# The second cross attention's scores moved from the head of a unit to the middle of the unit before

## The reference

```python
q = (query @ Wq.T + bq).reshape(N, Lq, HEADS, HEAD_DIM).transpose(0, 2, 1, 3)
k = (keys @ Wk.T + bk).reshape(N, Lk, HEADS, HEAD_DIM).transpose(0, 2, 1, 3)
v = (values @ Wv.T + bv).reshape(N, Lk, HEADS, HEAD_DIM).transpose(0, 2, 1, 3)
energy = jnp.einsum('bhqd,bhkd->bhqk', q, k)
energy = jnp.where(mask[:, None, None, :] == 0, jnp.float32(-1e+20), energy)
attention = jax.nn.softmax(energy / np.sqrt(HEAD_DIM), axis=-1)
out = jnp.einsum('bhqk,bhkd->bhqd', attention, v)
return out.transpose(0, 2, 1, 3).reshape(N, Lq, EMBED) @ Wo.T + bo
```

## Time and profile before

| | |
|---|---|
| median of three timed runs | 1763.58 us |
| span of the profiled execution | 1759.1 us |
| median less span | 4.5 us |
| TensorE busy | 1715.7 us, 98% of the span |
| layer 1's cross attention, first scores to last transpose | 1072.4 to 1303.4 us |

### The profile page before, as it was taken

One profiled execution on the slowest core, in us unless ns is written; L12 is line 12 of the kernel. 1 busy time (PEld: TensorE's weight loads), 2 busy tenths in 40 slices (PEclk: granted clock), 3 DMA queues, 4 the chain that ended last, 5 costly groups with the idle time before them and its releaser, 6 DMA issues.

```text
span 1759.1 us, 28411 instructions
## 1 busy us (share of the span) xinstructions
PE 1715.7 (98%) x11211; PEld 1315.8 (75%) x11211; DVE 910.5 (52%) x2029; ACT 716.4 (41%) x1564; POOL 238.3 (14%) x317
## 2 busy tenths in 40 slices
PE   7999999999999999999999999999999899999997
PEld 5677777777757666555999986777758587999997
DVE  4234344434346686523756564665564864455543
ACT  3333333333324436422655554555445442243432
POOL 0100000000003202422111031211101221121112
PEclk9999999999999999999999999999999999999999
DMA  6011010102042003025999961111231312788983
GB/s 248 25 73 48 25 48 25 49 25 96 1 156 96 1 1 144 23 99 214 375 390 390 384 200 60 37 37 31 79 144 35 155 59 96 317 329 325 327 326 94
DMA packets 43666, 245.87 MB, mean 140 GB/s; under 512 B 5786, under 2 KB 6290, under 8 KB 20481
## 3 DMA queue, kind: packets, MB, share of 16 engines
q1 hardware_dynamic: 31248, 215.91, 32.2%
q0 software_dynamic: 7664, 19.68, 4.0%
q10 hardware_dynamic: 4608, 8.33, 1.2%
HBM read 228.29 MB, written 16.13 MB: 139 GB/s over the span
## 4 chain that ended last, share of the span: by engine, by line
PE 92%; DVE 3%; issue 2%; DMA 1%; ACT 1%; POOL 1%; SPq 0%; POOLq 0%; DVEq 0%; ACTq 0%
PE bank L639 29%; PE bank L259 22%; PE bank L265 4%; PE bank L782 3%; PE bank L3284 3%; PE bank L810 3%; PE bank L1971 3%; PE bank L1973 3%; PE bank L1972 3%; PE bank L736 2%; PE bank L2773 2%; PE bank L1473 2%; PE bank L729 2%; PE bank L1157 2%; PE bank L1530 1%
## 5 line engine op out<-in xcount | busy, mean ns | idle before, releaser
L639 PE MATMUL bank<-split 128*128 128x512 f32 x2196 | 539.7, 398 | 0.8 <-ACT arena L665 0.8
L639 PEld LDWEIGHTS bank<-split 128*128 128x128 f32 x2196 | 401.9, 188 | 130.8 <-issue 21.7
L259 PE MATMUL bank<-arena,weights 128*128 128x128 f32 (+1 forms) x1992 | 244.7, 282 | 11.8 <-DMA weights<-in_L_xattn_w_kv 8.8
L259 PEld LDWEIGHTS bank<-arena,weights 128*128 128x128 f32 x1992 | 232.6, 192 | 25.2 <-issue 13.5
L753 DVE TENSOR_REDUCE small<-bank 128x1 f32<-128x512 f32 x64 | 43.9, 686 | 166.1 <-PE bank L729 166.1
L790 ACT COPY normed<-bank 128x512 f32<-128x512 f32 x128 | 68.9, 591 | 125.7 <-PE bank L782 125.7
L671 DVE COPY arena<-bank 128x512 f32<-128x512 f32 x76 | 52.4, 689 | 111.8 <-PE bank L639 111.8
L665 ACT COPY arena<-bank 128x512 f32<-128x512 f32 x76 | 44.6, 587 | 149.2 <-PE bank L639 116.0
L265 PE MATMUL bank<-weights,arena 128*128 128x512 f32 x224 | 102.9, 610 | 0.9 <-issue 0.9
L772 ACT ACTIVATE normed<-bank,small 128x512 f32<-128x512 f32 x64 | 44.1, 690 | 124.0 <-DVE small L755 123.7
L3390 DVE SCALAR_TENSOR_TENSOR arena<-bank,cols,arena 128x128 f32<-128x128 f32 x96 | 30.5, 349 | 114.5 <-issue 67.1
(11 more groups left out here) (397 smaller groups left out, 2915.8 us busy)
## 6 DMA issues: line engine op xcount, KB each, us to landing
weights<-in_L_ffn_re_w SPq DMA_DIRECT2D x62, 1024.0 KB, 8.2
weights<-in_L_w SPq DMA_DIRECT2D x20, 1408.0 KB, 11.0
arena<-in_ctxT SPq DMA_DIRECT2D x24, 1024.0 KB, 4.8
arena<-in_L_w SPq DMA_DIRECT2D x12, 1408.0 KB, 8.9
weights<-in_L_w_full SPq DMA_DIRECT2D x10, 1280.0 KB, 10.4
weights<-in_L_ffn_sw SPq DMA_DIRECT2D x9, 1024.0 KB, 4.9
expert_out<-arena ACTq DMA_DIRECT2D x31, 256.0 KB, 8.2
arena<-in_L_w_full SPq DMA_DIRECT2D x6, 1280.0 KB, 10.2
```

Of the source, the lines that this page charges most:

```text
L259: s = pe.matmul(out, w[:, k, j0:j0 + m], rhs(k), start=(k == 0), stop=(k == KT - 1))
L639: s = pe.matmul(bank[:, :], still, moving, start=(n == 0), stop=(n == len(order) - 1))
```

## The change

TensorE's order of issue alone changes, in layer 1 alone. The scores of unit 0 stand ahead of the loop. The scores of unit n + 1 are issued in unit n, behind the values of unit n - 1 and ahead of the second kv block and the turn of unit n. In layer 0 the scores stay where they were. The other engines' programs, the DMAs, the buffers and the number of instructions are as before.

```diff
@@ -840,8 +840,11 @@
 
             units = len(self.units)
             beside = units - (2 if self.layer == 0 else 3)
+            if self.layer == 1:
+                self.scores_tensor(pe, 0)
             for n, c, u, first, second, third, splits in self.plan:
-                self.scores_tensor(pe, n)
+                if self.layer == 0:
+                    self.scores_tensor(pe, n)
                 self.queries_tensor(pe, self.queries_beside(c, u))
                 for g in first:
                     self.kv_tensor(pe, *g)
@@ -851,6 +854,8 @@
                     project(n - beside)
                 if n >= 1:
                     self.values_tensor(pe, n - 1)
+                if self.layer == 1 and n + 1 < units:
+                    self.scores_tensor(pe, n + 1)
                 for g in second:
                     self.kv_tensor(pe, *g)
                 self.turn_tensor(pe, n)
```

## The result

The changed kernel takes 1758.93 us in the median of 10 runs (1754.85 to 1760.8), the kernel before 1763.75 us in as many (1761.37 to 1774.51). The ratio of the comparison is 0.9959, with a 95% interval from 0.9946 to 0.9971: faster by 7.2 us, between 5.1 and 9.5. The quotient of the two medians is 0.9973; both lie beyond 0.2%. Run again beside 23 runs of the kernel before, the changed kernel gave 0.9952 (0.9938 to 0.9967).

The account below looks back on a forecast made before the run. TensorE, busy 1715.7 of 1759.1 us, was taken as the bound. Savings of 6.2 + 0.9 = 7.1 us, with insertion and waits at zero, gave a span of 1752.0, plus 4.5 for the median: 1756.5 us, range 1754.5 to 1761.0.

Parts of the forecast that it names:

- What bounds the kernel: Layer 1's stage: TensorE busy for all 229.90 us, so only how tightly its blocks follow each other can change.
- Taking the scores out: Between turn and next block, 31 places: saves 0.24 us before kv (26), 0.18 before a float32 block (5), 7.1 us.
- Putting them in behind values: Scores after values in each unit: step out of values 0.58 us, scores 1.06 us, so no added cost.
- bound (+2.5, -1.6 us): Values into scores: 0.08 us more per unit, or 0.05 less if two array forms share part of their switch.
- The rule of the Trainium skill: Changing tiling mode drains TensorE: four changes a unit become three, one drain less in 31 units, estimated at 5.1 us.
- Unit 0: First unit: unit 1's scores cover the turn's 0.19 us softmax wait but split kv from turn; net 0.03 us won.
- The waits: Moved scores, turn, values, queries and keys in layer 1: all waits stay covered, cost 0; scores have 1.05 us of cover.
- Rival C: Scores wait for late maxima, holding back kv and turn: slower, middle 14 us, 1777 us; chance 0.03.
- Rival D: Behind the stage, more stretches at the lower clock give back 3.5 us: 1760.0 us; chance 0.06.

Follow-up runs that it names:

- full-array pair: The kernel before and the changed kernel, each with its scores matmuls on the full array instead of 64x128 halves; stages 244.50 and 244.34 us.
- scores before turn: Changed kernel with the scores of unit n + 1 moved behind the second kv block, ahead of the turn; stage 225.26 us, ratio 0.9971.

## Why the prediction was right, point by point

- *What bounds the kernel.* In the stage TensorE is busy without a pause, before and after. Right.
- *Taking the scores out.* 0.24 us a place with kv: the units shown give 0.23 and 0.21. 0.18 with a float32 block: the turn takes 0.93 for 1.02 (1288.05 - 1287.12 in the trace after) and the projection 3.53 (1291.58 - 1288.05) for 3.64 (1289.10 - 1285.46 in the trace before), 0.20. Sum 7.1 predicted, 6.92 measured, 0.22 for each of the 31. As the full-array pair shows, the split of a place's 0.24 us between turn and kv was not a reading that the rows allow; the sum was.
- *Putting them in behind values.* The value taken from values' other two followers, 0.58 and 1.06, was met. Neither bound (+2.5, -1.6 us) was needed. The full-array pair shows why: the cost goes with the change of form. The step from two measured followers to a third was an extrapolation, and it held.
- *The rule of the Trainium skill* (TensorEngine Tiling (Array Packing), section Key Properties: changing the tiling mode drains TensorE). The traces agree in kind: where the move takes away no change of form, 6.9 us became 0.16. The prediction's estimate of 5.1 us took the constant part of one matmul, from the Trainium skill's TensorE: Matmul & The Clock Gate, section Single matmul latency, for the price of a drain; it was low by 1.8 us. Prices read off the same neighbours fit better than one price per change, as the scores before turn showed.
- *Unit 0.* From its kv to the queries 4.94 us (1081.31 - 1076.37), before 5.08. Small, as worked out.
- *The waits.* None appeared. In the trace after, the second maximum is scaled at 1198.89 in the unit of 1197.15 and the next scores start at 1200.64: 1.75 us of cover where I had 1.05 as the least. The cover of the turn before the change was mis-sized, as 0.15 us; the second half's own wait makes it 0.64. This had no part in the sum.
- *Rival C* is real as a mechanism, but it cost nothing with 0.4 us of added work and 3.7 us in all with 1.4.
- *Rival D.* The profiled execution shows such a stretch behind the stage, 3.4 us, and so it met a sign that the prediction named for being wrong: a stage 7 us shorter in a span that is not. The runs answer it. The mean clock over all of them is no lower with the change, and span times clock has 6.7 us of the gain. The forecast of the median, 1756.5, was 2.4 us low all the same. It started from a median of three runs and one profile, and the ratio of the comparison puts the gain at 7.2 us. Why the stretches stand behind the stage in six of nine profiles with the move, and in none of three without, remains open.

## What to carry to other kernels

On an engine that never waits, look at the starts of its blocks, not at its busy time: blocks that use the array in different forms cost time at their borders, and bringing the odd ones together saves a border. The price can be read where the same neighbours stand elsewhere in the trace, as a sum over the blocks on both sides of the border. When a change is worth less than the program's own wander, measure it on the stretch that it touches, and look at the granted clock of both executions before two spans are compared. And a block that is moved may have covered a wait in the place that it leaves, as layer 0's first projection showed.

## What the runs showed of the hardware

- Between turn and kv, two scores matmuls of half the array each (1.06 us) cost 0.22 us more than beside values; as two full-array matmuls the place made no difference (244.50 against 244.34 us). The full-array scores made a unit 0.46 us longer than the half-array ones in the old order (244.50 against 229.87 us in 32 units) and 0.67 us in the new one (244.34 against 222.95), though they have fewer changes of form.
- A copy of a 128x512 float32 tile onto itself in SBUF took VectorE 0.43 us, one from PSUM (L671) 0.68 us.
- Runs of one kernel (scores before turn) had mean granted clocks from 0.989 to 0.998, and spans of the kernel before went from 1760.5 us at 0.998 to 1768.5 at 0.990.
